# A stencil's linear part moved into TensorE's scaled matrices, its squares to ScalarE, at the head of a four-layer kernel

## The chip, the cores and the metric

The kernel runs on one core of a Trainium2 chip. The metric is the device time of one execution in microseconds. The median of three runs of the kernel before is 1237.8 us.

## The reference

The input x is 2 batches of 1024 tokens of 256 features, float32. Four layers are added to it in turn:

```python
x = x + L0(x)   # stencil over tokens and features
x = x + L1(x)   # attention pooling over all tokens under a mask that a type id picks
x = x + L2(x)   # GELU network, 256 -> 1024 -> 256, 64 of the outputs by an expert per batch
x = x + L3(x)   # 8 gated experts and a shared one, 256 -> 1024 -> 256, silu(g) * u
```

The change is in L0. With reflection at the edges, lap_x is the sum of the two neighbours along the features less 2y, lap_y the same along the tokens, and per batch there are three scalars:

```python
du_dt = zX * lap_x + zY * lap_y + zR * y * (1.0 - y)
```

So x + L0(x) = zX (feature neighbours) + zY (token neighbours) + (1 - 2zX - 2zY + zR) x - zR x².

## The kernel before, in words

Features lie on the partitions, in DC = 2 chunks of 128; tokens lie along the free dimension, in blocks of 512 (two halves h to a batch). `xT` holds x so, and is overwritten layer by layer. Every engine has its own program, written out by hand in `nc.Block()`; the order of an engine's work is the order of the calls, and semaphores tie the engines together. There is no planner.

**Batch 0's stencil**, per half, before the change. `c0` is 1 - 2zX - 2zY + zR and `neg_zr` is -zR, both a number per partition (L658 to L661). ScalarE makes `poly` = c0 + neg_zr x (`stencil_poly`, L422 to L427). VectorE multiplies it by x (`stencil_square`, L677 to L681) and makes the sum of the token neighbours in `x_nb` (`stencil_tokens`, L683 to L697). TensorE makes the sum of the feature neighbours (`neighbours`, L1166 to L1173): `beside` holds four 128x128 matrices of ones, twos and zeros, which POOL fills with `affine_select` (L354 to L362), for each chunk c one matrix over its own chunk (index 2c) and one over the other chunk (2c+1), which has a single one in it, where the chunks meet. Both products of a chunk accumulate in one PSUM bank. VectorE adds zX times that bank to `poly` (`stencil_near`, L706 to L711) and zY times `x_nb` on top of it, into `xT` (`stencil_last`, L730 to L739, which signals `x1_done`). These are four operations of 128x1024 elements a half, two of them after the neighbour products. The calls stand at L898 to L905.

**Batch 1's stencil** has its neighbours summed by DMA and is done by VectorE between the GELU network's operations (table `between` at L935); it uses `c0`, `neg_zr` and `stencil_square` too.

**What follows for batch 0.** TensorE: after the neighbours, `score_layer(0, 0)` (waits for `x1_done`), some products of `ident` that keep it busy (`keep_warm`, after `v_wide` of POOL), `scores(0, 0)`, `score_layer(0, 1)`, `scores(0, 1)`, the transposes of x to tokens, and the pooled sums (L1175 to L1196). ScalarE makes tanh between `score_layer` and `scores` (L507 to L509). VectorE: `masks(0)`, `masked_scores(0, 0)`, `maxima`, two pieces of `fc_low`, `masked_scores(0, 1)` and then the softmax (L906 to L932). The dense network (L1240 on) starts when VectorE has split the first block of x in a high and a low part (`x2_low`), and L3 follows in a loop over the experts.

**Around the change.** POOL's order is: `ident`, `beside`, five memsets (L364 to L369) with no waits between them, six `affine_select` of the masks, and later the flags of the types and `v_wide` (L407). Before the neighbours TensorE multiplies `ident` by itself seven times (`WARM[0]`, L1176). SyncE loads x of batch 0 first, then weights, then batch 1 (L300 to L317). Each float32 product appears as two LDWEIGHTS and two MATMUL records.

Of the kernel before, what the change touches and what calls it, by code (L numbers as in the profile page):

```python
# [7 lines left out]
def stencil_attention_experts(nc, x_rows, scalars, types, expert_ids, w1, b1, v, fc1_w, fc1_b, fc2_w, fc2_b,  # L8
# [4 lines left out]
    ALU = mybir.AluOpType  # L13
    ACT = mybir.ActivationFunctionType
    AX = mybir.AxisListType.X

    P = 128
    B, S = x_rows.shape[1:]
    D = x_rows.shape[0] - 2
    DC = D // P  # L20
    T = B * S
    TB = 512
# [15 lines left out]
    GROUP = 32  # L38
# [4 lines left out]
    with ExitStack() as ctx:  # L43
# [3 lines left out]
        def sem(name):  # L47
            return ctx.enter_context(nc.semaphore(name))


        xT = sb("xT", [P, DC, T])
# [117 lines left out]
        SUMS = slice(KC, KC + KC * KC)  # L169

        beside_done = sem("beside_done")
        consts_done = sem("consts_done")
        types_done = sem("types_done")
        near_ps = sem("near_ps")
# [242 lines left out]
        def _(act):  # L417
# [3 lines left out]

            def stencil_poly(b, h):  # L422

                s0, s1 = (h * TB, (h + 1) * TB) if b == 0 else CUTS[h]
                act.wait_ge(x_in[b][h], 16)
                nc.scalar.activation(poly[:, b, :, s0:s1], xT[:, :, b * S + s0:b * S + s1], ACT.Identity,  # L426
                                     bias=c0[:, b:b + 1], scale=neg_zr[:, b:b + 1]).then_inc(poly_done, 1)  # L427

            def score_layer(b, h):
                act.wait_ge(attn_ps, b * NTB + h + 1)  # L430
# [64 lines left out]

            act.wait_ge(beside_done, 1)
            nc.scalar.activation(table_probe[:, :], ident[0:A, 0:1], ACT.Tanh)
            act.wait_ge(coef_done, 1)
            stencil_poly(0, 0)
            stencil_poly(0, 1)  # L500
            act.dma_start(fc1_bias[:, :], fc1_b).then_inc(bias_in, 16)
            for b in range(B):
                act.dma_start(out_bias[:, b, 0:1], fc2_b[0:P].unsqueeze(1)).then_inc(bias_in, 16)
# [134 lines left out]
        def _(dve):  # L638
            steps = [0]

            def link(ins):

                steps[0] += 1
                ins.then_inc(dve_step, 1)
                dve.wait_ge(dve_step, steps[0])
# [9 lines left out]


            dve.wait_ge(scal_in, 16)
            link(nc.vector.tensor_tensor(c0[:, :], sc_in[:, ZX:ZX + B], sc_in[:, ZY:ZY + B], ALU.add))  # L658
            link(nc.vector.tensor_scalar(c0[:, :], c0[:, :], -2.0, 1.0, ALU.mult, ALU.add))
            link(nc.vector.tensor_tensor(c0[:, :], c0[:, :], sc_in[:, ZR:ZR + B], ALU.add))  # L660
            nc.vector.tensor_scalar(neg_zr[:, :], sc_in[:, ZR:ZR + B], -1.0, None, ALU.mult).then_inc(coef_done, 1)  # L661

            def cut(b, h):
                return (h * TB, (h + 1) * TB) if b == 0 else CUTS[h]

            def gates():

# [7 lines left out]


            def stencil_square(b, h):  # L677
                s0, s1 = cut(b, h)
                part = poly[:, b, :, s0:s1]
                dve.wait_ge(poly_done, NTB * b + h + 1)  # L680
                link(nc.vector.tensor_tensor(part, part, xT[:, :, b * S + s0:b * S + s1], ALU.mult))  # L681
# [24 lines left out]
            def stencil_near(h):  # L706

                dve.wait_ge(near_ps, h + 1)
                part = poly[:, 0, :, h * TB:(h + 1) * TB]
                link(nc.vector.scalar_tensor_tensor(part, ps[:, NEAR_BANK + DC * h:NEAR_BANK + DC * (h + 1), :],  # L710
                                                    sc_in[:, ZX:ZX + 1], part, ALU.mult, ALU.add))  # L711

            def masks(b):
                if b == 0:
# [15 lines left out]
            def stencil_last(b, h):  # L730
                if b > 0:
                    dve.wait_ge(tokens_summed, 16)
                    edge, inner = ((0, 1), (S - 1, S - 2))[h]
                    link(nc.vector.tensor_scalar(x_nb[:, :, edge:edge + 1],
                                                 xT[:, :, b * S + inner:b * S + inner + 1], 2.0, None, ALU.mult))
                s0, s1 = h * TB, (h + 1) * TB
                nc.vector.scalar_tensor_tensor(xT[:, :, b * S + s0:b * S + s1], x_nb[:, :, s0:s1],  # L737
                                               sc_in[:, ZY + b:ZY + b + 1], poly[:, b, :, s0:s1],
                                               ALU.mult, ALU.add).then_inc(x1_done, 1)  # L739
# [156 lines left out]


            stencil_tokens(0, 0)  # L898
            stencil_square(0, 0)
            stencil_tokens(0, 1)  # L900
            stencil_near(0)
            stencil_last(0, 0)
            stencil_square(0, 1)
            stencil_near(1)
            stencil_last(0, 1)  # L905
            masks(0)  # L906
            masked_scores(0, 0)
            maxima(0, 0)
# [178 lines left out]
        def _(pe):  # L1087
            def mm(out_ap, lhsT, rhs, first, last, shared=False):
                return nc.tensor.matmul(out_ap, lhsT, rhs, start=first, stop=last, skip_group_check=shared)  # L1089
# [76 lines left out]
            def neighbours(h):  # L1166

                pe.wait_ge(x_in[0][h], 16)
                for c in range(DC):
                    bank = ps[:, NEAR_BANK + DC * h + c, :]  # L1170
                    for i, d in enumerate((c, 1 - c)):
                        last = mm(bank, beside[:, 2 * c + i, :], xT[:, d, h * TB:(h + 1) * TB], i == 0, i == DC - 1)
                last.then_inc(near_ps, 1)  # L1173

            pe.wait_ge(beside_done, 1)  # L1175
            keep_warm(WARM[0])  # L1176
            pe.wait_ge(beside_done, 1 + 2 * DC)
            neighbours(0)
            neighbours(1)
            pe.wait_ge(w1_in, 48)  # L1180
# [211 lines left out]
```

## Time and profile before

| what | value |
|---|---|
| median of three runs | 1237.8 us (1236.59 to 1239.88) |
| time of the profiled execution | 1236.2 us |
| its span, first to last instruction | 1234.0 us |
| TensorE busy with matmuls | 1219.7 us, 99% |
| TensorE loading weights | 993.3 us, 80% |
| VectorE busy | 871.6 us, 71% |
| ScalarE busy | 637.4 us, 52% |
| POOL busy | 14.9 us, 1% |

The span is 2.2 us shorter than the execution's own time. A busy engine is not always the bound: matmuls overlap, and the share is a mean over stages. The stencil of batch 0 takes place in the first 17 us of the span.

### The profile page before, as it was taken

How to read it: one execution, taken by the hardware profiler on the slowest of the kernel's cores; microseconds unless marked ns; L12 is line 12 of the kernel's file. 1: busy time of each engine (PE TensorE's matmuls, PEld its weight loads, DVE VectorE, ACT ScalarE, POOL GpSimd, SP SyncE). 2: the span in 40 equal slices, each digit the busy share in tenths (PEclk: the TensorE clock that was granted, in tenths of full speed). 3: DMA queues.
4: the chain of work that ended last, by engine and by line, in shares of the span. 5: the costliest groups of instructions: out<-in, count | busy, mean ns of one | idle time of the engine just before them, and what ended most of it. 6: DMA issues, size and time to landing. Idle time of an engine off the chain costs nothing.

```text
span 1234.0 us, 16072 instructions
## 1 busy us (share of the span) xinstructions
PE 1219.7 (99%) x5386; PEld 993.3 (80%) x5386; DVE 871.6 (71%) x1479; ACT 637.4 (52%) x1060; POOL 14.9 (1%) x40
## 2 busy tenths in 40 slices
PE   8999999999999999999999999999999999999998
PEld 4678788888888888888888888888888888888886
DVE  8757686777577767776776687668757875777555
ACT  4655664554455545544554455445545554454443
POOL 4000000000000000000000000000000000000000
PEclk9999999999999999999999999999999999999999
DMA  8311010011001101010101010001000100010000
GB/s 233 61 52 37 28 39 1 26 39 39 1 27 38 38 0 38 25 38 0 38 25 38 0 51 25 25 0 51 25 25 12 51 25 13 13 38 1 17 17 35
DMA packets 20542, 39.75 MB, mean 32 GB/s; under 512 B 7074, under 2 KB 8610, under 8 KB 20386
## 3 DMA queue, kind: packets, MB, share of 16 engines
q1 hardware_dynamic: 19088, 37.30, 9.9%
q0 software_dynamic: 544, 2.10, 0.9%
q8 instruction: 13, 0.21, 0.1%
q10 hardware_dynamic: 882, 0.02, 0.0%
q14 instruction: 15, 0.12, 0.0%
HBM read 37.31 MB, written 2.10 MB: 32 GB/s over the span
## 4 chain that ended last, share of the span: by engine, by line
PE 92%; DVE 5%; ACT 1%; issue 1%; DMA 0%; DVEq 0%; ACTq 0%
PE ps L1089 92%; DVE h_lo L980 1%; DVE w_lo L871 0%; DVE fcw_lo L726 0%; DVE poly L681 0%; ACT poly L426 0%; DVE x_lo L854 0%; DMA sc_in<-in_scalars 0%; ACT stage L553 0%; DVE xT L737 0%; DVE poly L710 0%; DVE x_dn L786 0%; DVE chunk_max L762 0%; ACT h_hi L557 0%; DVE x_dn L757 0%
## 5 line engine op out<-in xcount | busy, mean ns | idle before, releaser
L1089 PE MATMUL ps<-xc_hi,w_hi 128*128 128x512 f32 x1008 | 392.6, 389 | 1.0 <-DVE ps L1009 0.8
L1089 PE MATMUL ps<-xc_lo,w_hi 128*128 128x512 f32 x1008 | 392.2, 389 | 0.0
L1089 PE MATMUL ps<-xc_hi,w_lo 128*128 128x512 f32 x1008 | 392.2, 389 | 0.0
L590 ACT ACTIVATE silu<-ps 128x512 f32<-128x512 f32 x144 | 86.2, 599 | 325.2 <-PE ps L1089 325.2
L1089 PE MATMUL ps<-h_hi,w_hi 128*128 128x512 f32 x576 | 224.4, 390 | 0.9 <-DVE h_lo L995 0.5
L1089 PE MATMUL ps<-h_hi,w_lo 128*128 128x512 f32 x576 | 224.1, 389 | 0.0
L1089 PE MATMUL ps<-h_lo,w_hi 128*128 128x512 f32 x576 | 224.1, 389 | 0.0
L1089 PEld LDWEIGHTS ps<-xc_hi,w_hi 128*128 128x128 f32 x1008 | 189.2, 188 | 42.0 <-DVE ps L1009 1.2
L1089 PEld LDWEIGHTS ps<-xc_hi,w_lo 128*128 128x128 f32 x1008 | 189.2, 188 | 39.4
L1089 PEld LDWEIGHTS ps<-xc_lo,w_hi 128*128 128x128 f32 x1008 | 189.2, 188 | 39.1
L995 DVE TENSOR_TENSOR h_lo<-hidden,h_hi 128x512 fp32r<-128x512 f32 x144 | 99.7, 692 | 145.1 <-ACT h_hi L604 145.1
L1021 DVE TENSOR_TENSOR u_sum<-ps,p_copy 128x512 f32<-128x512 f32 x144 | 98.9, 687 | 97.0 <-PE ps L1089 97.0
L569 ACT ACTIVATE ps<-ps 128x512 f32<-128x512 f32 x144 | 83.8, 582 | 136.1 <-PE ps L1089 136.1
L1009 DVE TENSOR_TENSOR ps<-ps,p_copy 128x512 f32<-128x512 f32 x144 | 100.7, 700 | 40.7 <-PE ps L1089 40.7
L1089 PEld LDWEIGHTS ps<-h_hi,w_hi 128*128 128x128 f32 x576 | 108.1, 188 | 24.3 <-DVE h_lo L995 1.2
L1089 PEld LDWEIGHTS ps<-h_hi,w_lo 128*128 128x128 f32 x576 | 108.1, 188 | 22.5
L1089 PEld LDWEIGHTS ps<-h_lo,w_hi 128*128 128x128 f32 x576 | 108.1, 188 | 22.4
L583 ACT ACTIVATE silu<-ps 128x512 f32<-128x512 f32 x144 | 86.1, 598 | 60.8 <-PE ps L1089 60.7
L1028 DVE TENSOR_TENSOR hidden<-silu,u_sum 128x512 f32<-128x512 f32 x144 | 99.7, 693 | 15.0
L1015 DVE TENSOR_TENSOR h_lo<-hidden,h_hi 128x512 fp32r<-128x512 f32 x144 | 98.4, 683 | 0.9 <-ACT h_hi L597 0.7
L1002 DVE TENSOR_TENSOR hidden<-silu,ps 128x512 f32<-128x512 f32 x144 | 97.9, 680 | 0.0
L871 DVE TENSOR_TENSOR w_lo<-piece,w_hi 128x1152 fp32r<-128x1152 f32 x72 | 97.3, 1351 | 0.0
(141 smaller groups left out, 1002.6 us busy)
## 6 DMA issues: line engine op xcount, KB each, us to landing
piece<-in_moe_w SPq DMA_DIRECT2D x72, 384.0 KB, 3.1
out_x<-xT SPq DMA_DIRECT2D x8, 256.0 KB, 2.4
xT<-in_x_rows SPq DMA_DIRECT2D x2, 528.0 KB, 5.3
raw<-in_fc_w SPq DMA_DIRECT2D x1, 1024.0 KB, 7.5
x_up<-in_x_rows SPq DMA_DIRECT2D x1, 1024.0 KB, 9.3
x_up<-in_x_rows POOLq DMA_DIRECT2D x1, 1024.0 KB, 9.1
x_nb<-in_x_rows SPq DMA_DIRECT2D x1, 1022.0 KB, 12.4
x_nb<-in_x_rows POOLq DMA_DIRECT2D x1, 1022.0 KB, 10.6
```

The lines of the kernel that those rows point to most:

```text
L569: nc.scalar.activation(ps[:, BANK_B + i % 2, :], ps[:, BANK_A, :], ACT.Copy).then_inc(seeded, 1)
L583: nc.scalar.activation(silu0[:, i % 2, :], ps[:, BANK_A, :], ACT.Silu).then_inc(silu0_done, 1)
L590: nc.scalar.activation(silu1[:, :], ps[:, BANK_E, :], ACT.Silu).then_inc(silu1_done, 1)
L871: nc.vector.tensor_tensor(w_lo[k][:, :, :], piece[:, k % RAWS, A11:RT, :], w_hi[k][:, :, :].bitcast(f32), ALU.subtract).then_inc(wlo_done, 1)
L980: nc.vector.tensor_tensor(h_lo[:, k % RING, :], stage[:, n % PAIR, :], h_hi[:, k % RING, :].bitcast(f32), ALU.subtract).then_inc(fc_h_read ...
L995: nc.vector.tensor_tensor(h1_lo[:, :], hidden1[:, :], h1_hi[:, :].bitcast(f32), ALU.subtract).then_inc(h1_ready, 1)
L1002: nc.vector.tensor_tensor(hidden0[:, :], silu0[:, i % 2, :], ps[:, BANK_B + i % 2, :], ALU.mult).then_inc(hidden0_done, 1)
L1009: nc.vector.tensor_tensor(ps[:, BANK_E, :], ps[:, BANK_B + i % 2, :], p5_copy[:, :], ALU.add).then_inc(g1_seeded, 1)
L1015: nc.vector.tensor_tensor(h0_lo[:, i % 2, :], hidden0[:, :], h0_hi[:, i % 2, :].bitcast(f32), ALU.subtract).then_inc(h0_ready, 1)
L1021: nc.vector.tensor_tensor(u_sum[:, :], ps[:, BANK_B + i % 2, :], p5_copy[:, :], ALU.add).then_inc(u1_done, 1)
L1028: nc.vector.tensor_tensor(hidden1[:, :], silu1[:, :], u_sum[:, :], ALU.mult).then_inc(hidden1_done, 1)
L1089: return nc.tensor.matmul(out_ap, lhsT, rhs, start=first, stop=last, skip_group_check=shared)
```

## The change

- VectorE waits for all of `beside` to be filled. It multiplies the four matrices by zX, makes c0 as before, and adds c0 times `ident` to the two own-chunk matrices. Then it signals `beside_scaled`, which TensorE's neighbours now wait for, and makes `neg_zr`.
- ScalarE computes x² of each half straight from `xT` into `poly`, as soon as x has landed, with no coefficient.
- VectorE's `stencil_near` makes zY times `x_nb` plus the PSUM bank, in `x_nb`; a new `stencil_end` adds `neg_zr` times `poly` and writes `xT`. The squares of batch 0 on VectorE are gone, so a half has three operations. The token sums of both halves come first.
- TensorE's product over the other chunk takes the 32 rows only that hold the one: rows 0 to 31 for chunk 0, rows 96 to 127 for chunk 1. The two come one after the other, behind the two own-chunk products.

```diff
@@ ScalarE
-                s0, s1 = (h * TB, (h + 1) * TB) if b == 0 else CUTS[h]
+                s0, s1 = CUTS[h]
...
+            def stencil_square(h):
+
+                act.wait_ge(x_in[0][h], 16)
+                nc.scalar.activation(poly[:, 0, :, h * TB:(h + 1) * TB], xT[:, :, h * TB:(h + 1) * TB],
+                                     ACT.Square).then_inc(poly_done, 1)
...
             nc.scalar.activation(table_probe[:, :], ident[0:A, 0:1], ACT.Tanh)
+            stencil_square(0)
+            stencil_square(1)
             act.wait_ge(coef_done, 1)
-            stencil_poly(0, 0)
-            stencil_poly(0, 1)
@@ VectorE
             dve.wait_ge(scal_in, 16)
+            dve.wait_ge(beside_done, 1 + 2 * DC)
+            link(nc.vector.tensor_scalar(beside[:, :, :], beside[:, :, :], sc_in[:, ZX:ZX + 1], None, ALU.mult))
             link(nc.vector.tensor_tensor(c0[:, :], sc_in[:, ZX:ZX + B], sc_in[:, ZY:ZY + B], ALU.add))
             link(nc.vector.tensor_scalar(c0[:, :], c0[:, :], -2.0, 1.0, ALU.mult, ALU.add))
             link(nc.vector.tensor_tensor(c0[:, :], c0[:, :], sc_in[:, ZR:ZR + B], ALU.add))
+            own_rows = beside[:, :, :].rearrange("p (c i) m -> p c i m", i=2)[:, :, 0, :]
+            nc.vector.scalar_tensor_tensor(own_rows, ident[:, :].unsqueeze(1).to_broadcast([P, DC, P]), c0[:, 0:1],
+                                           own_rows, ALU.mult, ALU.add).then_inc(beside_scaled, 1)
             nc.vector.tensor_scalar(neg_zr[:, :], sc_in[:, ZR:ZR + B], -1.0, None, ALU.mult).then_inc(coef_done, 1)
...
             def stencil_near(h):
 
                 dve.wait_ge(near_ps, h + 1)
-                part = poly[:, 0, :, h * TB:(h + 1) * TB]
-                link(nc.vector.scalar_tensor_tensor(part, ps[:, NEAR_BANK + DC * h:NEAR_BANK + DC * (h + 1), :],
-                                                    sc_in[:, ZX:ZX + 1], part, ALU.mult, ALU.add))
+                part = x_nb[:, :, h * TB:(h + 1) * TB]
+                link(nc.vector.scalar_tensor_tensor(part, part, sc_in[:, ZY:ZY + 1],
+                                                    ps[:, NEAR_BANK + DC * h:NEAR_BANK + DC * (h + 1), :],
+                                                    ALU.mult, ALU.add))
+
+            def stencil_end(h):
+                dve.wait_ge(coef_done, 1)
+                dve.wait_ge(poly_done, h + 1)
+                nc.vector.scalar_tensor_tensor(xT[:, :, h * TB:(h + 1) * TB], poly[:, 0, :, h * TB:(h + 1) * TB],
+                                               neg_zr[:, 0:1], x_nb[:, :, h * TB:(h + 1) * TB],
+                                               ALU.mult, ALU.add).then_inc(x1_done, 1)
...
             stencil_tokens(0, 0)
-            stencil_square(0, 0)
             stencil_tokens(0, 1)
             stencil_near(0)
-            stencil_last(0, 0)
-            stencil_square(0, 1)
+            stencil_end(0)
             stencil_near(1)
-            stencil_last(0, 1)
+            stencil_end(1)
@@ TensorE
                 for c in range(DC):
-                    bank = ps[:, NEAR_BANK + DC * h + c, :]
-                    for i, d in enumerate((c, 1 - c)):
-                        last = mm(bank, beside[:, 2 * c + i, :], xT[:, d, h * TB:(h + 1) * TB], i == 0, i == DC - 1)
+                    mm(ps[:, NEAR_BANK + DC * h + c, :], beside[:, 2 * c, :], xT[:, c, h * TB:(h + 1) * TB], True, False)
+                for c in range(DC):
+                    edge = (slice(0, GROUP), slice(P - GROUP, P))[c]
+                    last = mm(ps[:, NEAR_BANK + DC * h + c, :], beside[edge, 2 * c + 1, :],
+                              xT[edge, 1 - c, h * TB:(h + 1) * TB], False, True)
                 last.then_inc(near_ps, 1)
...
-            pe.wait_ge(beside_done, 1 + 2 * DC)
+            pe.wait_ge(beside_scaled, 1)
             neighbours(0)
             neighbours(1)
```

## Rows read from the trace of the kernel before

**Rows 1.** The page: the chain that ended last, shares by engine.

```profile
PE 92%; DVE 5%; ACT 1%; issue 1%; DMA 0%; DVEq 0%; ACTq 0%
```

**Rows 2.** The view of the cores: span and mean granted TensorE clock.

```profile
core 0: 1234.0 us, clock 1.000
```

**Rows 3.** Timeline of VectorE: start us, us, engine, line, operation, tiles, shapes.

```profile
4.05 0.17 DVE L659 TENSOR_SCALAR c<-c 128x2 f32<-128x2 f32 x1
...
4.48 1.58 DVE L661 TENSOR_SCALAR neg_zr<-sc_in 128x2 f32<-128x2 f32 x1
...
5.27 1.22 DVE L696 TENSOR_TENSOR x_nb<-xT 128x1022 f32<-128x1022 f32 x1
...
7.45 1.23 DVE L681 TENSOR_TENSOR poly<-poly,xT 128x1024 f32<-128x1024 f32 x1 [0.96 <-ACT poly L426]
...
10.03 1.28 DVE L710 SCALAR_TENSOR_TENSOR poly<-ps,sc_in,poly 128x1024 f32<-128x1024 f32 x1
...
11.35 1.28 DVE L737 SCALAR_TENSOR_TENSOR xT<-x_nb,sc_in,poly 128x1024 f32<-128x1024 f32 x1
...
15.13 1.28 DVE L737 SCALAR_TENSOR_TENSOR xT<-x_nb,sc_in,poly 128x1024 f32<-128x1024 f32 x1
...
17.60 0.69 DVE L757 TENSOR_TENSOR x_dn<-ps,blend 128x512 f32<-128x512 f32 x1
...
20.73 0.68 DVE L757 TENSOR_TENSOR x_dn<-ps,blend 128x512 f32<-128x512 f32 x1
```

**Rows 4.** Timeline of POOL around the memsets, and of its selects.

```profile
4.14 0.55 POOL L349 TENSOR_SCALAR_AFFINE_SELECT beside<-beside 128x128 f32<-128x128 f32 x2
4.63 0.22 POOL L364 MEMSET ones<- 128x128 f32 x1
...
5.43 0.61 POOL L369 MEMSET blend_src<- 128x600 f32 x1
6.18 0.45 POOL L349 TENSOR_SCALAR_AFFINE_SELECT blend_src<-blend_src 128x128 f32<-128x128 f32 x1
...
7.33 1.49 POOL L349 TENSOR_SCALAR_AFFINE_SELECT blend_src<-blend_src 128x64 f32<-128x64 f32 x2
...
14.06 0.39 POOL L407 TENSOR_TENSOR v_wide<-ones,v_sb 64x128 f32<-64x128 f32 x1
```

**Rows 5.** TensorE: neighbour and ident products grouped by line, then its timeline.

```profile
L1089 PE MATMUL ps<-xT,beside x16: 592/592/863, 5.3 to 12.0; 128*128 128x512 f32 x16
...
L1089 PE MATMUL ps<-ident x14: 421/421/579, 2.0 to 4.9; 128*128 128x128 f32 x14
...
6.00 0.19 PEld L1089 LDWEIGHTS ps<-xT,beside 128*128 128x128 f32 x1 [0.24 <-issue]
...
12.78 1.90 PE L1089 MATMUL ps<-xT,w_sb 128*64 128x512 f32 x4 [0.18 <-DVE xT L737]
...
14.62 0.94 PE L1089 MATMUL ps<-ident 128*128 128x128 f32 x6
...
15.52 1.12 PE L1089 MATMUL ps<-x_dn,v_wide 64*128 64x512 f32 x2
...
16.57 1.93 PE L1089 MATMUL ps<-xT,w_sb 128*64 128x512 f32 x4
...
19.35 1.10 PE L1089 MATMUL ps<-x_dn,v_wide 64*128 64x512 f32 x2
...
35.91 0.47 PE L1089 MATMUL ps<-x_hi,fcw_hi 128*128 128x512 f32 x1 [0.90 <-DVE x_lo L854]
```

**Rows 6.** Timeline of ScalarE: first polynomial, tanh of half 0.

```profile
6.10 1.24 ACT L426 ACTIVATE poly<-xT,c,neg_zr 128x1024 f32<-128x1024 f32 x1 [2.33 <-DVE neg_zr L661]
...
14.78 0.68 ACT L431 ACTIVATE x_dn<-ps,b_sb 64x512 f32<-64x512 f32 x1 [1.21 <-PE ps L1089]
```

**Rows 7.** The chain of waits from 40 us on: start us, us, what.

```profile
47.65 4.88 PE ps L1089 x16
...
53.40 16.92 PE ps L1089 x62
```

More of the change, by code:

```diff
@@ L171, in stencil_attention_experts @@
         beside_done = sem("beside_done")
+        beside_scaled = sem("beside_scaled")
         consts_done = sem("consts_done")
@@ L660, in _ @@
             link(nc.vector.tensor_tensor(c0[:, :], c0[:, :], sc_in[:, ZR:ZR + B], ALU.add))
+            own_rows = beside[:, :, :].rearrange("p (c i) m -> p c i m", i=2)[:, :, 0, :]
+            nc.vector.scalar_tensor_tensor(own_rows, ident[:, :].unsqueeze(1).to_broadcast([P, DC, P]), c0[:, 0:1],
+                                           own_rows, ALU.mult, ALU.add).then_inc(beside_scaled, 1)
             nc.vector.tensor_scalar(neg_zr[:, :], sc_in[:, ZR:ZR + B], -1.0, None, ALU.mult).then_inc(coef_done, 1)
-            def cut(b, h):
-                return (h * TB, (h + 1) * TB) if b == 0 else CUTS[h]
             def gates():
@@ L677, in stencil_square @@
             def stencil_square(b, h):
-                s0, s1 = cut(b, h)
+                s0, s1 = CUTS[h]
                 part = poly[:, b, :, s0:s1]
```

## The prediction

> **What bounds the kernel now.** I read the page first, then the chain of waits, then the timelines of the first 36 us. The page has the chain that ended last 92% on TensorE [rows 1] over a span of 1234.0 us [rows 2], so a change of the opening acts only by moving the moment from which TensorE is the bound. The chain in order of time shows that moment: from 47.65 us on TensorE carries it in long pieces, 62 matmul records in one of them [rows 7]. Ahead of it VectorE carries nearly everything: it works almost without a gap from 7.45 us to the masked scores of half 1 at 20.73 us [rows 3], and the first matmul of the dense stage starts at 35.91 us, released by VectorE's `x_lo` [rows 5].
>
> So the quantity to forecast is when VectorE can start the second `masked_scores(0, 1)`, now 20.73 us. Two paths meet there. VectorE's own: `stencil_last(0, 1)` ends at 15.13+1.28=16.41, the masks fill the time to 17.60, `masked_scores(0, 0)` starts there, and 3.13 us later the second [rows 3]. TensorE's: the neighbour matmuls, `score_layer(0, 0)` at 12.78, tanh from 14.78 to 15.46, `scores(0, 0)` at 15.52, `score_layer(0, 1)` at 16.57, `scores(0, 1)` from 19.35 to 20.45 [rows 5, 6]. TensorE's path is only 20.73-20.45=0.28 us shorter. That is the main thing to see: VectorE may save microseconds, and 0.28 us of it count unless TensorE is earlier too. From 20.73 us on I take every shift to be carried to the end, since the work up to 47.65 us hangs together by short waits.
>
> **VectorE, what goes.** Two squares of 1.23 us, with the semaphore that ties each to the next operation: 2.5 us. The near and last operations stay two a half, 1.28 us each [rows 3], with other operands. TensorE's matrices carry zx and the linear term c0, so ScalarE needs no coefficients: it squares x as soon as x has landed. ScalarE's activation took 1.24 us and started at 6.10, 2.33 us after its wait began, on `neg_zr` [rows 6]. The squares should be ready by 6.5 and 7.8 us and the first is wanted after 11 us: price zero, covered by VectorE's token sums, and if that cover were gone at most the 1.24 us. The same for the constants' DMAs issued behind them.
>
> **VectorE, what comes.** The scaling of `beside` (128x512) and the fused multiply-add of `own_rows` (128x256). Neither has a row. The first is bounded below by nothing wider than a 128x2 operation, 0.17, and above by the two-input operation of that size, 0.69 for the masked scores [rows 3]; I take 0.45 to 0.5 us, nearer the upper end, as the elements are the same and only the second input is missing. The second lies between the same ends; at the rate of 1022 elements in 1.22 us [rows 3] it is 0.17+256 x 1.03 ns=0.43.
>
> **The wait that is added.** VectorE now waits for five increments of `beside_done`. POOL's last select ends at 4.14+0.55=4.69 us [rows 4], where VectorE began its coefficients before 4.05 [rows 3]. Everything on VectorE stands behind it, the token sums too, and TensorE waits for `beside_scaled` instead of the selects. And the multiply is a one-input tensor_scalar on SBUF, just when POOL runs its memsets. What such an operation meets there stands in the trace: the 128x2 multiply into `neg_zr`, begun at 4.48, took 1.58 us and ended at 6.06, where L659, the same kind, took 0.17 [rows 3]; POOL's chain of selects and five memsets ends at 5.43+0.61=6.04 [rows 4]. The two-input sum at 5.27 took its plain 1.22 meanwhile. I read it as VectorE held until the chain ends.
>
> So: multiply issued 4.8, held to 6.04, ended 6.5. Three small c0 operations at about 0.2 us spacing: 7.1; some 0.15 more where a tensor_scalar meets one select (0.45 us at 6.18, [rows 4]): 7.25. Fused operation: 7.7. TensorE starts at **7.75**, where it now starts at 5.3 [rows 5]. The unknown hold is bounded on both sides: no hold gives 6.45; held behind the whole series of six selects (about 0.29 us each by the four from 6.18 to 7.33, so to 8.2, and 0.7 for what follows) gives 8.9.
>
> **TensorE.** The sixteen neighbour records start from 5.3 to 12.0; the second one's weights load at 6.00 [rows 5], so the first kept the array 0.70 us and the other spacings are (12.0-6.0)/14=0.43. The diff replaces four full products by two full ones and two of 32 rows a half, each of the same 512 columns. I cost them at the same slot, since the products with a contraction of 64 rows also show two records, over 1.12 and 1.10 us, no less than full ones take [rows 5]; rival 1 bounds this from below, and above it I add nothing but half a record a half for a change of form, inside the range. TensorE leaves the neighbours 7.0 us after its start: 14.75. From `score_layer(0, 0)` to the end of `scores(0, 1)` it took 20.45-12.78=7.67; of these about 0.15 were a wait for VectorE's xT ahead of 16.57, which is over by then: 7.5. That gives 22.25, and `masked_scores(0, 1)` at 22.3. The warm-up products on `ident` and the wait for `v_wide` (14.06+0.39=14.45, [rows 4]) fit inside the tanh's time.
>
> VectorE in the same case: `neg_zr` 7.9, two token sums 10.5, near 11.8, end 13.1; near of half 1 waits for TensorE's 14.95, end 17.5; masks 18.7; the second masked scores could be at 21.85. TensorE's path decides. **Sum: 22.3-20.73=+1.5 us**; VectorE's 2.5 us become idle time. The profiled execution took 1236.2 us, 1.6 below the median of 1237.8 (three runs, 1236.59 to 1239.88). On the median: 1239.3. About 0.3%, 3.7 us, is what a measurement of this kernel tells from no change, so this is no difference.
>
> The transfer of `x_nb` behind x1_done is no term: x1_done comes 1.1 us later at most, and its first user, `stencil_last(1, 0)`, works just ahead of `score_layer(1, 0)` at 47.65 [rows 7]. If it were late after all, that 1.1 us is its price.
>
> **Rivals.**
> 1. The 32-row products run side by side. The neighbours then take between 0.45 and 0.9 us less a half, and `score_layer(0, 0)` can start at 13.35 (bound by end(0) on VectorE) to 13.85: 20.9 to 21.4, +0.2 to +0.7, **1238.3**. Against it: no row shows two products at once. The Trainium skill (TensorEngine Tiling (Array Packing), "Key Properties") says both that different tiles can run in parallel and that a change of tiling mode drains the engine, and no run here shows either yet. 20%.
> 2. The multiply is not held (the memsets hold only what they held by chance, or pass it in a gap): start 6.45, 21.0, +0.3, **1238.1**. For it: L659 passed at 4.05. Against: the 1.58 us. 15%; with rival 1 as well VectorE's saving shows and it is -1, **1236.8**, 5%: even then not faster by 0.3%.
> 3. The small tensor_scalar behind the multiply is held by the six selects too: start 8.9, 23.45, +2.7, **1240.5**. Against it: the sum of 1.23 us at 7.45 entered that series unharmed, and it was POOL's select that waited (1.49 us for two, [rows 4]). The Trainium skill (SBUF — State Buffer, "SBUF: two separate sides") says that VectorE in a 2-port mode and GpSimd take a shared port pair exclusively, for a whole instruction; by it the 1.58 us are plain, and whether the selects let VectorE in between two of them is left open. 12%.
> 4. The slower side: TensorE's clock. The granted clock is 1.000 in the record [rows 2], yet the opening `ident` products follow one another by about 0.22 us (14 of them from 2.0 to 4.9) where six later ones took 0.94 in all, about 0.10 apart, and the first neighbour record is the longest, 863 against 592 ns [rows 5]: first at the level of 1.2 GHz, then of 2.4, with the change inside that record. After the change TensorE is idle from the end of the `ident` products until 7.75, just where the rise fell. If the rise is put off, each neighbour record done before it costs 0.43 more: with four records hit +1.7+1.5, **1241.0**; with all sixteen +8.4, **1246.2**. It decides from the sixth slow record, (3.7-1.5)/0.43. Against it: activity up to 5.1 is the same as now. 12%, half of it beyond 0.3%.
>
> **How the numbers follow.** Forecast 36%, rivals 20, 20, 12, 12. Predicted: 1239.3. The range from 1236.6 to 1241.8 takes in all starts from 6.45 to 8.9, side by side or not, and the mild form of rival 4. Only the strong form of it is over 3.7 us, with a little for run-to-run spread: slower 7%. No case reaches 3.7 us below: faster 1%. Within 0.3%: 92%.
>
> **What would show it.** Right: the `beside` multiply takes about 1.6 us and ends near 6.5; the first xT,beside record starts near 7.75; sixteen records 0.43 apart; ScalarE's squares done by 8; near of half 1 with a wait for TensorE; masked scores at 22.3; the first dense matmul at 37.4. Wrong: a start under 7, records of a pair starting together (rival 1), spacing of 0.86 (rival 4), or a first dense matmul that doesn't follow the masked scores' shift, by which my carrying it to the end would fall.

## The result, and the profile after

The changed kernel took 1242.11 us in the median of 20 runs (1236.42 to 1245.07), the kernel before 1237.88 (1236.2 to 1239.88): ratio 1.0026 with a 95% interval of 1.0015 to 1.0036. That is slower by about a quarter of a per cent, 3.2 us by the ratio and 4.2 by the medians, still inside the 3.7 us that the prediction called no difference when the ratio is taken, but clear of zero. The profiled execution took 1243.46 us, 7.3 more than the one of before.

What to notice first is the spread. Six of the 20 executions took 1236.4 to 1238.4 us, with a mean granted clock of 0.999 or 1.000; the other fourteen took 1240.2 to 1245.1, with 0.991 to 0.997. Only two of the six lie at 1236.4 to 1236.6, beside the fastest of the kernel before at 1236.2. The kernel before spreads too, but to 1239.9 at most: the change made the time depend more on TensorE's clock.

The view of the cores, and the page's shares of the chain that ended last, after (95% TensorE for [rows 1]'s 92%: the opening's chain now runs through TensorE too):

```profile
core 0: 1241.3 us, clock 0.997
...
PE 95%; DVE 3%; ACT 1%; issue 1%; POOL 0%; DVEq 0%; POOLq 0%; ACTq 0%
```

The timeline of VectorE after, the rows that answer to [rows 3] (start us, us, engine, line, operation):

```profile
4.79 1.51 DVE L666 TENSOR_SCALAR beside<-beside,sc_in 128x512 f32<-128x512 f32 x1 [4.79 <-POOL beside L350]
...
6.53 0.20 DVE L668 TENSOR_SCALAR c<-c 128x2 f32<-128x2 f32 x1
...
7.00 0.48 DVE L671 SCALAR_TENSOR_TENSOR beside<-ident,c,beside 128x256 f32<-128x256 f32 x1
...
7.58 1.21 DVE L705 TENSOR_TENSOR x_nb<-xT 128x1022 f32<-128x1022 f32 x1
...
13.44 1.28 DVE L719 SCALAR_TENSOR_TENSOR x_nb<-x_nb,sc_in,ps 128x1024 f32<-128x1024 f32 x1 [3.32 <-PE ps L1104]
...
14.76 1.29 DVE L726 SCALAR_TENSOR_TENSOR xT<-poly,neg_zr,x_nb 128x1024 f32<-128x1024 f32 x1
...
17.92 1.28 DVE L719 SCALAR_TENSOR_TENSOR x_nb<-x_nb,sc_in,ps 128x1024 f32<-128x1024 f32 x1 [1.88 <-PE ps L1104]
...
19.24 1.28 DVE L726 SCALAR_TENSOR_TENSOR xT<-poly,neg_zr,x_nb 128x1024 f32<-128x1024 f32 x1
...
21.80 0.69 DVE L774 TENSOR_TENSOR x_dn<-ps,blend 128x512 f32<-128x512 f32 x1
...
25.54 0.69 DVE L774 TENSOR_TENSOR x_dn<-ps,blend 128x512 f32<-128x512 f32 x1 [0.53 <-PE ps L1104]
```

The multiply of `beside` took 1.51 us and ended at 6.30, near the 6.5 that the prediction had from `neg_zr`'s 1.58; that is 0.28 after the last memset, where the prediction allowed about 0.46. The fused operation ended at 7.48. From there on VectorE waits for TensorE: 3.32 us before the first `stencil_near`, 1.88 before the second.

POOL after, as [rows 4]: memsets to 6.02, and the six selects behind them, which did not hold the small c0 operation (0.20 us).

```profile
5.41 0.61 POOL L370 MEMSET blend_src<- 128x600 f32 x1
6.17 2.77 POOL L350 TENSOR_SCALAR_AFFINE_SELECT blend_src<-blend_src 128x128 f32<-128x128 f32 x6
```

TensorE after, as [rows 5]: first the records on `beside` grouped by line (duration min/median/max, first and last start), then the timeline.

```profile
L1104 PE MATMUL ps<-xT,beside x16: 587/1061/1222, 7.5 to 17.3; 128*128 128x512 f32 x8, 32*128 32x512 f32 x8
...
8.55 1.91 PE L1104 MATMUL ps<-xT,beside 128*128 128x512 f32 x2
...
9.40 1.92 PE L1104 MATMUL ps<-xT,beside 128*128 128x512 f32 x2
...
10.26 1.06 PE L1104 MATMUL ps<-xT,beside 128*128 128x512 f32 x1
...
11.25 1.22 PE L1104 MATMUL ps<-xT,beside 32*128 32x512 f32 x2
...
12.26 1.06 PE L1104 MATMUL ps<-xT,beside 32*128 32x512 f32 x2
...
17.80 1.93 PE L1104 MATMUL ps<-xT,w_sb 128*64 128x512 f32 x4
...
25.34 0.94 PE L1104 MATMUL ps<-v_sb,x_dn 64*128 64x1 f32 x8
...
26.22 3.25 PE L1121 MATMUL ps<-ident,xT 128*128 128x128 f32 x16
...
41.81 0.47 PE L1104 MATMUL ps<-x_hi,fcw_hi 128*128 128x512 f32 x1 [0.68 <-DVE x_lo L871]
...
78.46 1.94 PE L1104 MATMUL ps<-v_sb,x_dn 64*128 64x1 f32 x16
```

Three things are in these rows. The start at 7.54 is near the forecast's 7.75. The full records then follow one another by 0.85 us (8.55, 9.40, 10.26), twice the 0.43 of before: the lower level, 1.2 GHz. And the 32-row records start two at a time (11.25 and 12.26, x2 each, 0.006 us apart in the trace): four records in the time of two. The neighbours are left at 17.80, not at 14.75; the second masked scores start at 25.54 (before 20.73, +4.8), the first dense product at 41.81 (before 35.91, +5.9).

The 1.1 us between these last two shifts, and what is lost later, are in the view of windows (us busy with counts by engine, then granted clock, DMA share, GB/s):

```profile
26.00:27.00 1.00, 1.00 (x9) 0.98 (x9) 0.97 (x3) 0.00 (x0) 0.00 (x0) 0.85 0.92 303
27.00:28.00 1.00, 1.00 (x7) 1.00 (x6) 0.93 (x3) 0.20 (x1) 0.88 (x1) 0.50 0.95 339
...
80.00:82.00 2.00, 2.00 (x10) 1.69 (x10) 1.97 (x4) 0.70 (x2) 0.00 (x0) 0.83 0.00 0
82.00:84.00 2.00, 2.00 (x7) 1.52 (x6) 1.83 (x7) 0.00 (x0) 0.00 (x0) 0.50 0.00 0
84.00:86.00 2.00, 2.00 (x9) 1.62 (x8) 1.39 (x4) 0.94 (x2) 0.00 (x0) 0.82 0.00 0
```

The clock drops to 0.50 from 26.7 to 30.1 and from 81.3 to 84.7. The first drop lies on the transposes of x, 3.25 us for 16 records where they took 1.97 in the kernel before:

```profile
21.16 1.97 PE L1106 MATMUL ps<-ident,xT 128*128 128x128 f32 x16
```

The span grew by 7.3 us: 5.9 up to the first dense product and 1.4 behind it, where the second drop is the only one up to the kernel's end. In the opening this view shows 1.00 although the spacing is that of the lower level. The trace's first record of the granted clock begins only at 16.5 us (in the kernel before at 5.7); ahead of it the view has nothing to show and says 1.00, and the spacing is what to read. Both drops begin just behind score-column products, matmuls with a single column (64x1): eight records that ended at 26.3, sixteen that ended at 80.4.

Nobody waited for ScalarE's squares. The first ended at 6.29 (forecast 6.5); the second ended at 8.57, not 7.8, since its half of x landed only at about 7.5, but it was not wanted before 19.2:

```profile
5.23 1.06 ACT L433 ACTIVATE poly<-xT 128x1024 f32<-128x1024 f32 x1 [1.47 <-DMA xT<-in_x_rows]
...
7.51 1.06 ACT L433 ACTIVATE poly<-xT 128x1024 f32<-128x1024 f32 x1 [1.22 <-DMA xT<-in_x_rows]
```

### The profile page after: what moved, and what is told of

It reads as the page before. It is cut to its first block, busy times and chain, and to the rows that moved or that the text cites. A ratio compares the mean times of both kernels' runs of the same rounds, so it can differ in the third digit from the quotient of the medians.

```text
span 1241.3 us, 16072 instructions
## 1 busy us (share of the span) xinstructions
PE 1225.6 (99%) x5386; PEld 995.6 (80%) x5386; DVE 871.2 (70%) x1479; ACT 636.9 (51%) x1060; POOL 13.1 (1%) x40
## 4 chain that ended last, share of the span: by engine, by line
PE 95%; DVE 3%; ACT 1%; issue 1%; POOL 0%; DVEq 0%; POOLq 0%; ACTq 0%
PE ps L1104 94%; DVE w_lo L888 0%; PE ps L1121 0%; DVE h_lo L995 0%; DVE x_lo L871 0%; DVE fcw_lo L743 0%; ACT stage L560 0%; ACT poly L427 0%; POOL beside L350 0%; DVE beside L666 0%; ACT h_hi L564 0%; DVE hidden L1043 0%; DVE h_lo L1030 0%; DVE hidden L1017 0%; DVE u_sum L1036 0%
```

## The experiments

Each ratio is against the kernel before in the same runs (its medians there: 1237.8 to 1238.1 us, its fastest executions 1236.1 to 1236.3). It is not the quotient of the two medians. The executions of most kernels here fall in groups one or two microseconds apart, and a median jumps from one group to the next, so the fastest executions are given beside it.

**The gap bridged.** The changed kernel with more products of `ident` ahead of the neighbours:

```diff
-    WARM = [7, 3]
+    WARM = [14, 3]
```

> The changed kernel with 14 products of ident instead of 7 ahead of the neighbours, so that TensorE has work up to about 7 us. Clock theory (the idle stretch from 5.35 to 7.53 us keeps TensorE at the lower level, and with it all sixteen neighbour records 0.85 us apart): the neighbour records follow one another by 0.43, the last of them ends near 13 instead of 17.8, the granted clock of the execution is 1.000 in nearly every run, and the time is 1236.0 to 1237.5. Late-start theory (the start at 7.53 instead of 5.30 costs by itself, the clock is a side matter): neighbours still in time for no gain over 1 us, time at 1240 or more.

Median 1238.00 us, ratio 1.0000 (0.9991 to 1.0010). Its records on `beside`, and its first dense product:

```profile
L1104 PE MATMUL ps<-xT,beside x16: 587/592/697, 7.5 to 13.0; 128*128 128x512 f32 x8, 32*128 32x512 f32 x8
...
13.47 1.93 PE L1104 MATMUL ps<-xT,w_sb 128*64 128x512 f32 x4
...
21.21 0.69 DVE L774 TENSOR_TENSOR x_dn<-ps,blend 128x512 f32<-128x512 f32 x1 [0.53 <-PE ps L1104]
...
36.38 0.48 PE L1104 MATMUL ps<-x_hi,fcw_hi 128*128 128x512 f32 x1 [0.71 <-DVE x_lo L871]
```

The start is still 7.5, the median record 592 ns instead of 1061, and the neighbours are left at 13.47 instead of 17.80. With nothing but work to bridge the idle stretch, the change's whole loss is gone, and the trace's first record of the granted clock begins at 6.3 us instead of 16.5. The clock theory holds. The median is 0.5 us above the expected range, and a clock of 1.000 in nearly every run was too much to expect: five of 11 executions had it, at 1236.40 to 1236.56, the others 0.997 to 0.999, as many executions of the kernel before have too.

**The gap alone.** The kernel before with one more wait:

```diff
             pe.wait_ge(beside_done, 1 + 2 * DC)
+            pe.wait_ge(x_in[0][1], 16)
             neighbours(0)
```

> The kernel before with one wait more: TensorE's neighbours wait for the second half of x too, which lands at about 7.5 us, where the changed kernel starts its neighbours; the 7 products of ident end near 5.3 as they do now. Nothing else of the change is in it. Clock theory: the neighbour records follow one another by 0.85, leaving them (sixteen in a row, none paired) near 21, and the time is 6 to 9 us over the kernel before, with a clock under 1.000 in most runs. Late-start theory: spacing 0.43, last record ends near 14.6, time +1 to +2 us.

Median 1241.05, ratio 1.0028 (1.0017 to 1.0039): as slow as the whole change, with no other part of it in the kernel.

```profile
L1089 PE MATMUL ps<-xT,beside x16: 592/592/1193, 7.5 to 16.0; 128*128 128x512 f32 x16
```

The sixteen records start from 7.5 to 16.0, 0.57 apart on average: slow at first, at the upper level later. The rise came within the neighbours (first clock record at 11.6 us), which I had not expected so early; hence +3.5 us and not 6 to 9.

**The gap bridged in the kernel before.** The same wait, with 14 products of `ident`.

> The kernel of the gap (neighbours of the kernel before started only once the second half of x has landed) with 14 products of ident instead of 7. It separates the late start from the clock. Clock theory: spacing 0.43, time +1 to +2 us over the kernel before (by the prediction's sum for TensorE's path: a start at 7.5, scores of half 1 ended near 22, +1.4). If the gap alone costs as much as the unbridged one, the clock theory falls.

Median 1239.64, ratio 1.0014 (1.0005 to 1.0023).

```profile
L1089 PE MATMUL ps<-xT,beside x16: 592/592/667, 7.5 to 14.1; 128*128 128x512 f32 x16
...
22.31 0.69 DVE L757 TENSOR_TENSOR x_dn<-ps,blend 128x512 f32<-128x512 f32 x1 [0.19 <-PE ps L1089]
```

From 7.5 to 14.1 the spacing is 6.6/15=0.44, and the second masked scores start at 22.31. So the late start by itself is worth 1.7 us, as expected, and the same start without the bridge another 1.7. The two intervals overlap slightly (1.0023 and 1.0017), but the executions whose clock was 1.000 do not: 1237.91 to 1238.45 here, 1240.54 to 1241.05 with the gap alone. Late start and late rise cost about the same here, and the pairs of 32-row records pay for most of the first.

**When the clock rose.** The traces of all the kernels in this document, those further down too, bear this out. In the nine whose opening has no long idle stretch ahead of the neighbours, the trace's first record of the granted clock begins at 4.9 to 7.7 us. In the four with an idle stretch of 1.5 to 2.2 us it begins at 10.7 (the kernel of "The hold"), 11.6 (the gap alone), 13.3 (the full rows in the changed kernel) and 16.5 us (the changed kernel). Each trace is of one execution, so within the four the order may be chance.

**The 32-row products.** First in the changed kernel, then in the bridged one, the other chunk's product over all 128 rows:

```diff
-                    edge = (slice(0, GROUP), slice(P - GROUP, P))[c]
-                    last = mm(ps[:, NEAR_BANK + DC * h + c, :], beside[edge, 2 * c + 1, :],
-                              xT[edge, 1 - c, h * TB:(h + 1) * TB], False, True)
+                    last = mm(ps[:, NEAR_BANK + DC * h + c, :], beside[:, 2 * c + 1, :],
+                              xT[:, 1 - c, h * TB:(h + 1) * TB], False, True)
```

> The changed kernel with the other chunk's product over all 128 rows again instead of 32; everything else of the change stays. If the 32-row products of the two chunks run side by side (the trace has two records starting together, 11.25 and 12.26), this one is slower by two records a half: at 0.85 spacing up to +3.4 us, less where the clock has risen meanwhile, so +1 to +3 us over the changed kernel. If they only share the record's form: no difference.

Median 1241.66, ratio 1.0034 (1.0023 to 1.0044) beside the changed kernel's 1.0026 (1.0015 to 1.0036): the intervals overlap, and nothing can be told. Its profiled execution, 1240.44, had the clock up from 13.3 us, the changed kernel's only from 16.5, though both start alike (records at 7.5, 8.5, 9.4 and 10.3). When the clock rises differs from one execution to the next, it seems, and hides the pairs.

> The changed kernel with 14 products of ident and the other chunk's product over all 128 rows: the case that the prediction summed (start near 7.5, sixteen records 0.43 apart, clock up). If that sum holds: neighbours left near 14.5, second masked scores at 22.1 to 22.3, time +1.5 us over the kernel before, 1239.2. If the 32-row products run in pairs, the bridged kernel with them, 1238.0, is the faster by what the pairs save at the upper clock level: 0.46 us a half by its spacings (2.97 us a half against 8 x 0.43), so 0.9 us.

At the upper level they show. This is also the case that the prediction summed. Median 1238.05, which is 1.15 below the expected 1239.2, ratio 1.0011 (1.0002 to 1.0020); the fastest execution took 1237.61 against 1236.40 of the bridged kernel with pairs.

```profile
L1104 PE MATMUL ps<-xT,beside x16: 592/592/595, 7.7 to 14.2; 128*128 128x512 f32 x16
...
11.43 1.28 DVE L719 SCALAR_TENSOR_TENSOR x_nb<-x_nb,sc_in,ps 128x1024 f32<-128x1024 f32 x1 [1.30 <-PE ps L1104]
...
14.69 1.93 PE L1104 MATMUL ps<-xT,w_sb 128*64 128x512 f32 x4
...
22.43 0.69 DVE L774 TENSOR_TENSOR x_dn<-ps,blend 128x512 f32<-128x512 f32 x1 [0.53 <-PE ps L1104]
```

Neighbours left at 14.69 and second masked scores at 22.43, against 13.47 and 21.21 with pairs: 1.2 us, of which 0.2 is a later start here (7.73 for 7.53). A half takes 3.48 us with full records and 2.97 with pairs, so the pairs save some 0.5 us a half, not the 0.86 of two records. The two medians are almost equal (1238.05 and 1238.00). In each kernel five of 11 executions had a clock of 1.000: 1237.61 to 1237.77 here, 1236.40 to 1236.56 with pairs, and a median falls just behind them.

**VectorE's saving.** The bridged kernel with one operation more a half:

```diff
             def stencil_end(h):
+                link(nc.vector.tensor_tensor(x_up[:, 0, :, 0:TB], x_nb[:, :, h * TB:(h + 1) * TB],
+                                             x_nb[:, :, h * TB:(h + 1) * TB], ALU.mult))
                 dve.wait_ge(coef_done, 1)
```

> The bridged kernel (14 products of ident) with one operation of 128x1024 elements more on VectorE a half, between near and end, about 1.25 us each, whose result nobody reads: the fourth operation is back. If VectorE's saving lies in idle time, as the prediction has it (TensorE's scores set the second masked scores), the first extra operation delays end(0) and with it the first score layer by about 1.1 us and the second is hidden: between 0 and +1.3 us. If VectorE's path is the bound: +2.5 us, 1240.5.

Median 1240.73, ratio 1.0023 (1.0014 to 1.0032), more than its 2.5 us. But the fastest execution, 1238.11, is only 1.7 above the bridged kernel's, which is still 0.4 over the first expectation's upper end. The timeline of the profiled execution, which took 1242.2:

```profile
12.01 1.23 DVE L724 TENSOR_TENSOR x_up<-x_nb 128x1024 f32<-128x1024 f32 x1
...
14.87 3.42 PE L1106 MATMUL ps<-xT,w_sb 128*64 128x512 f32 x4 [1.32 <-DVE xT L728]
```

The score layer starts at 14.87 instead of 13.47: the first extra operation delays it by 1.4, the second is hidden. TensorE idled 1.32 us before it, and its four records then took 3.42 us where the same four take 1.93: the clock again, at the lower level from 15.1 to 18.5 us. So with pairs an operation in this place counts for 1.4 us, and the further loss, up to the median, goes with the clock. The place matters: the squares of the kernel before stood ahead of the two near operations, where VectorE now waits for TensorE (0.57 and 0.30 us in the bridged kernel, 1.30 and 0.77 with full rows), and no run put the operation there. So the run is likely to overstate what the saving is worth.

**The hold.** The changed kernel with 7 products of `ident` again, and the scaling as a two-input product:

```diff
-            link(nc.vector.tensor_scalar(beside[:, :, :], beside[:, :, :], sc_in[:, ZX:ZX + 1], None, ALU.mult))
+            link(nc.vector.tensor_tensor(beside[:, :, :], beside[:, :, :],
+                                         wide(sc_in[:, ZX:ZX + 1], 2, [P, 2 * DC, P]), ALU.mult))
```

> The changed kernel (7 products of ident) with the scaling of beside written as a two-input product (0.69 us by the masked scores' row), so that POOL's memsets don't hold it: TensorE's neighbours start at 6.7 instead of 7.53. Clock theory: the idle stretch is 1.35 us instead of 2.2; if that is short enough, the neighbours run 0.43 apart and the time is 1237 to 1238 with clock 1.000; if not, it stays at 1240 to 1242. Theory that the hold is a matter of the one-input form: the operation ends near 5.5. If it still ends near 6.3, the hold has another cause.

Median 1235.79, ratio 0.9992 (0.9982 to 1.0001).

```profile
4.78 0.69 DVE L666 TENSOR_TENSOR beside<-beside,sc_in 128x512 f32<-128x512 f32 x1 [4.78 <-POOL beside L350]
...
L1105 PE MATMUL ps<-xT,beside x16: 587/692/1222, 6.8 to 14.1; 128*128 128x512 f32 x8, 32*128 32x512 f32 x8
```

0.69 us at the same moment and under the same memsets, where the one-input form took 1.51: the hold belongs to that form. TensorE starts at 6.82. The fastest executions of the kernel before in these runs took 1236.15, 0.4 us more; the ratio's interval just includes no difference. That is better than the 1237 to 1238 expected. Six of 11 executions took 1235.73 to 1235.79, the rest 1237.6 to 1239.5. The profiled one, at 1237.65, is of the second kind: sixteen records from 6.8 to 14.1, longer than the 5.5 us of the bridged kernel's: the first six start ahead of the clock record, which begins at 10.7, and are spaced as at the lower level, although the mean granted clock reads 1.000. An idle stretch of 1.5 us thus put the rise off in this execution. By their times the six at 1235.73 to 1235.79 escaped it, but none of those has a trace.

**A version to beat both.** c0 made before the wait for `beside`, the two-input scaling, and 9 products of `ident`:

```diff
-    WARM = [7, 3]
+    WARM = [9, 3]
...
             dve.wait_ge(scal_in, 16)
+            link(nc.vector.tensor_tensor(c0[:, :], sc_in[:, ZX:ZX + B], sc_in[:, ZY:ZY + B], ALU.add))
+            link(nc.vector.tensor_scalar(c0[:, :], c0[:, :], -2.0, 1.0, ALU.mult, ALU.add))
+            link(nc.vector.tensor_tensor(c0[:, :], c0[:, :], sc_in[:, ZR:ZR + B], ALU.add))
             dve.wait_ge(beside_done, 1 + 2 * DC)
...
```

> A version to beat both kernels: c0 is made before the wait for beside, the scaling is the two-input product, and 9 products of ident bridge the rest. TensorE's neighbours start at 6.0 to 6.1, 0.43 apart, in pairs over 32 rows, left at 12.0; second masked scores 19.7 to 20.0 instead of 20.73; time 1 us under the kernel before, 1236.8, if the shift is carried to the end as in the other runs. Late-start theory and clock theory agree here; a time of 1237.8 or more would say that VectorE's path has become the bound.

The opening came out as expected: neighbours from 6.05, left at 11.99, second masked scores at 19.73. The time is harder to read. The median of 1236.83 is the expected number, but the ratio is 1.0000 (0.9991 to 1.0009). Five executions took 1236.6 to 1236.8, five 1238.5 to 1238.8, and one 1234.93. The first dense product, and the windows around 74 us:

```profile
34.91 0.47 PE L1105 MATMUL ps<-x_hi,fcw_hi 128*128 128x512 f32 x1 [0.71 <-DVE x_lo L872]
...
71.52 1.94 PE L1105 MATMUL ps<-v_sb,x_dn 64*128 64x1 f32 x16
...
74.19 0.61 PE L1105 MATMUL ps<-h_hi,fcw_hi 128*128 128x512 f32 x1
...
73.00:74.00 1.00, 1.00 (x8) 0.90 (x8) 0.96 (x3) 0.76 (x2) 0.00 (x0) 1.00 0.00 0
74.00:77.00 3.00, 3.00 (x9) 2.37 (x8) 2.83 (x8) 0.00 (x0) 0.00 (x0) 0.53 0.00 0
```

The product at 34.91 is 1.0 us earlier than 35.91, but none of the 11 executions had a clock of 1.000, and 34.91+1197.8, the distance that the bridged kernel has, would be a span of 1232.7 and not the 1234.4 of this one. Only the execution of 1234.93, with a span of 1232.8, got there. The drop stands behind sixteen score-column records (64x1), which begin at 71.52.

The other traces have the same pattern. Leaving out the kernels' last microseconds, all the traces here hold eleven drops. Ten begin 0 to 0.9 us after a group of score columns has ended: five behind batch 0's eight records, five behind batch 1's sixteen. The eleventh is the one at 15.1 us with VectorE's extra operation, behind an idle stretch. But the same products also stand in the traces that have no drop. And in the four traces that have both drops the second begins 51.2 us after the end of the first, to 0.01 us, while the columns end 0.2 to 0.9 us ahead of it. So the products alone do not decide whether and when the clock falls.

**Taking the score columns apart.** The same version with TensorE's `score_columns(1, 1)` one place later in the dense stage, and VectorE's exponents with it:

```diff
-                       (1, 2): [lambda: score_columns(1, 0), lambda: score_columns(1, 1)],
+                       (1, 2): [lambda: score_columns(1, 0)],
+                       (1, 3): [lambda: score_columns(1, 1)],
...
-                       (1, 2): [lambda: outer_exponents(1), lambda: inner_exponents(1, 0),
-                                lambda: inner_exponents(1, 1)],
-                       (1, 3): [lambda: gates()],
+                       (1, 2): [lambda: gates()],
+                       (1, 3): [lambda: outer_exponents(1), lambda: inner_exponents(1, 0),
+                                lambda: inner_exponents(1, 1)],
```

> The version with c0 first, the two-input scaling and 9 products of ident, and in the dense stage batch 1's score columns apart: one half after up(2) of block 1, the other after up(3), VectorE's exponents one place later. In the run without this, the granted clock was 0.50 from about 74 us on, right behind sixteen records of 64x1 (1.94 us in a row), and its first dense product at 34.91 instead of 35.91 was not seen in the time. If those records' low activity brings the clock down, the drop goes, the clock is 1.000 and the time is 1235.0 to 1235.5 in most runs. If the drop comes from the phase of the clock's measure alone, it stays in about as many runs, 1236.6 and 1238.7.

Median 1234.87, ratio 0.9984 (0.9974 to 0.9995): faster than the kernel before, and its interval lies below that of the changed kernel. Nine of 12 executions took 1234.8 to 1235.3.

```profile
core 0: 1232.7 us, clock 0.999
...
70.00:80.00 10.00, 10.00 (x52) 7.69 (x50) 7.78 (x21) 6.58 (x10) 0.00 (x0) 1.00 0.00 0
...
34.94 0.47 PE L1105 MATMUL ps<-x_hi,fcw_hi 128*128 128x512 f32 x1 [0.70 <-DVE x_lo L872]
```

The first dense product is where it was, and the window from 70 to 80 us is at 1.00. The expected clock of 1.000 is 0.999 here; what is missing lies behind 1230 us, where TensorE has no work left, and costs nothing:

```profile
1230.00:1232.70 2.70, 0.00 (x0) 0.00 (x0) 0.00 (x0) 0.00 (x0) 0.00 (x0) 0.66 0.52 194
```

The other way, two products of `ident` after each half of the columns, left in one place:

```diff
-                       (1, 2): [lambda: score_columns(1, 0), lambda: score_columns(1, 1)],
+                       (1, 2): [lambda: score_columns(1, 0), lambda: keep_warm(2),
+                                lambda: score_columns(1, 1), lambda: keep_warm(2)],
```

> The same version, with two products of ident after each half of batch 1's score columns instead of moving them: four products, eight records, about 0.5 us of TensorE's time. If low activity there brings the clock down: fewer runs with a drop, fast ones at 1235.4 to 1235.8, 0.5 us above what the split would give. If it doesn't: 0.5 us more than the version without, 1237.2.

Median 1237.97, ratio 1.0001 (0.9992 to 1.0010), the fastest 1236.14: a miss, above even the second expectation. Nine of 11 executions still had 0.998 or 0.999. In the profiled one the opening itself was the late part (clock up only from 7.7 us, a drop at 21.4 behind batch 0's score columns, first dense product at 37.13). Around the treated products, from 73.7 to 76.4 us, it has no drop, but one trace is little, and the times say that the products of `ident` did not help.

**The split alone**, in the kernel before:

> The kernel before with nothing but the split of batch 1's score columns. It tells how much of the split version's 1234.87 us is the split and how much the earlier opening. If the opening's 1.0 us (first dense product at 34.91 for 35.91) is the gain and the split only keeps it: this one stays at 1236.1 to 1237.8. If the split is the gain: 1235.0 to 1235.5.

Median 1236.43, ratio 0.9989 (0.9980 to 0.9998), the fastest five 1236.08 to 1236.16. The first expectation named the right size for the opening (the fastest executions go from 1236.1 here to 1234.8 with the earlier opening, 1.3 us), and missed that the split gains by itself. It leaves the fastest executions where they were and thins out the longer ones: one of 11 took over 1237.2 us here, 13 of 15 of the kernel before in the same runs. That it does so by taking away drops is likely but not shown, since the profiled execution of the kernel before has none. By the ratios the split is worth 0.11% and both together 0.16%; those intervals overlap.

## Why the prediction was right or wrong

**The path and the sum** were right. TensorE's path, not VectorE's, set the second masked scores, and VectorE's first near waited for TensorE in the changed, the bridged and the full-row kernels. The case that the prediction called likeliest was built as the bridged kernel with full rows: start 7.73 (forecast 7.75), neighbours left 14.69 (14.75), second masked scores 22.43 (22.3). Its time is +1.4 us by the ratio 1.0011 and +1.5 by the fastest executions (forecast +1.5), though nothing by the medians. The terms hold to 0.15 us each, apart from the multiply behind its hold, which took 0.28 us and not 0.46.

**The hold** was right: 1.51 us, ended at 6.30 for a forecast of 6.5. With the two-input form there is no hold, so it belongs to the one-input form. Rival 2 (no hold) did not happen, and rival 3 (the selects hold the c0 operation too) did not: 0.20 us in a series of selects. The Trainium skill (SBUF — State Buffer, "SBUF: two separate sides") has the shared pair taken for a whole instruction. Beside the memsets the trace agrees, though VectorE stood here until the last of several overlapping ones had ended (6.02). Beside the selects it shows no such hold: the small operation ran its 0.20 us from 6.53 although the trace has selects without a gap there.

**Carried to the end** was right: the shift of the second masked scores and of the first dense product agree within 0.1 us wherever the clock stays up between them (+0.48 and +0.47 in the bridged kernel, -1.0 and -1.0 in the last version), and reach the span unless a drop intervenes.

**Cost of the 32-row products** was wrong: "I cost them at the same slot". They run two at a time, rival 1, for which I gave 20% and 0.45 to 0.9 us a half; measured 0.5 at the upper level.

**The clock** was the step that failed. The sum took 0.43 us for each of sixteen records, with the argument "activity up to 5.1 is the same as now". It is the same, and was not enough: in the kernel before, TensorE went on with the neighbours from 5.3, and the rise came at 5.7, inside their first record. With the idle stretch the full records ran at 0.85, and rival 4 is what most executions are. By the number it is its mild form (1241.0), by the mechanism in the profiled execution nearly the strong one: the clock rose at 16.5 us, when twelve of the sixteen records had begun. I gave it 12% as an either-or; in fact both happen, fourteen executions against six, and of the six only two reach the fast end. That the range still held the result is therefore partly luck: pairs, which the sum did not have, paid back part of a clock loss that it did not have either. Two things were missing in it. The neighbours' loss, 17.80-14.75=3.05 us, is partly paid back by rival 1. And the clock drops again at 26.7 and 81.3 us, which no case of mine had, and which go with 1.1 and 1.4 us of the profiled execution.

**VectorE's 2.5 us** as idle time agrees with the waits of the full-row trace (1.30 and 0.77 us before the two near operations), but no run put the operations back there. With pairs 1.4 us of them count when the operation stands behind near; how much at the squares' old place is open.

The range was right by the ratio (1.0026 x 1237.88=1241.1, high 1241.8), and the median of 1242.11 lies 0.3 above it. The 7% for slower by over 0.3% look too few: the interval reaches 1.0036.

Left open: why the clock rises at different moments in executions of the same kernel, and why the score columns are followed by a drop in some executions and not in others. In two kernels the split in two groups leaves fewer executions with a drop's extra time; the products of `ident` after each group did not, so low activity alone is not shown to be the reason.

## What to carry to other kernels

When an operation is put between TensorE's warm-up and its first real work, the warm-up has to be lengthened with it: here seven tiny products more were worth as much as the change had lost. What to look at is the spacing of the records: the mean granted clock read 1.000 in an execution that lost 1.9 us to a late rise. Before counting what an engine saves, find the other path into the same wait and how far behind it is (0.28 us here). And compare executions one by one, with their clocks: a median over executions with and without a drop hid 1.2 us between two versions here, and the drops swallowed an opening that was 1.0 us earlier.

## What the runs showed of the hardware that was not expected

- A one-input tensor_scalar on VectorE stood under POOL's memsets for 1.2 us (1.51 for 128x512), the two-input product of the same size and moment took 0.69 us: the form that I had priced below the other is the slower one beside the memsets.
- Two products of 32 rows each, at rows 0 to 31 and 96 to 127 and into two PSUM banks, start together, with no flag. The Trainium skill (TensorEngine Tiling (Array Packing), "Key Properties") says that tiles can run in parallel and that a change of mode drains the engine. The first shows: x2 at one start. The second is not told apart: the starts around a change are 0.52 us apart where full records are 0.43, but so are the two pairs of a half, with no change between them (0.53, or 1.01 for 0.85 at the lower level). In all a pair costs (2.97-4 x 0.43)/2 = 0.63 us at the upper level.
- An idle stretch of 2.2 us on TensorE, ahead of the rise of the clock, put it off from inside the first neighbour record (5.7 us) to 16.5 us in the profiled execution, after 8.9 us of matmuls one behind the other; with 1.5 us of idle time 5 of 11 executions took the longer time.
- Ten of eleven drops of the clock in these traces begin within 0.9 us after a group of 64x1 products has ended. With batch 1's sixteen split in two groups of eight, nine of 12 executions stayed at the fast end (1234.8 to 1235.3); with the sixteen together, one of 11 (1234.93).
- The view of the granted clock shows 1.00 in stretches where the spacing of the records is that of 1.2 GHz, when they lie ahead of the first recorded change.
